# Two more receptances made early, four weight corrections moved to DMA, and mixing tables made one unit later

## The chip, the cores and the metric

The kernel runs on one core of one Trainium2 chip. Its metric is the device time of one execution in microseconds (us).

## The reference, cut to what matters

The input x has 2 sequences of 2048 times and 256 channels, 4096 tokens in all. All is in fp32. `F` stands for 512, the shared expert's width; there are 8 experts of width 256, and each token goes to the two of highest gate score.

```python
xn = layernorm(x)                                   # without scale and shift
k, v = xn @ key_w.T, xn @ value_w.T                 # time mixing
r = sigmoid(xn @ recep_w.T)                         # the "receptance"
# scan over time, per channel, state (aa, bb, pp):
#   wkv_t = (e1 * aa + e2 * v_t) / (e1 * bb + e2 + 1e-6)
#   e1, e2 from time_first and pp alone; the state decays by time_decay
mixed = (r * wkv) @ out_w.T
scores = softmax(xn @ gate_w.T + gate_b)            # 8 experts, top 2
expert_e(t) = (silu(t @ w1_e.T + b1_e) * (t @ w3_e.T + b3_e)) @ w2_e.T + b2_e
shared(t) = silu(t @ ws1.T + bs1) * (t @ ws3.T + bs3) @ ws2.T + bs2
out = x + mixed + sum of the two experts' results by their scores + shared(xn)
```

The scan as written never uses k, so its denominators and decay factors do not depend on x. They are tables over time and channel, which the kernel makes once: the mixing tables.

## The kernel before, in words

**Tiling.** The tokens are cut into 8 *steps* of 512 (256 times of both sequences). An fp32 product is made as three products of reduced-precision parts: each operand is cut into a high part (a rounding copy, by ScalarE) and a low part (what the rounding left, a subtraction, mostly by VectorE). "Cutting" below means this. A plain fp32 matmul exists too; `early_column` (L381) uses it.

**Three stages** follow each other, each with one stream of instructions for each engine: `route`, `run_experts`, `mix`. TensorE, VectorE, ScalarE, POOL and SP (which issues most DMAs) run their own streams in order and meet at semaphores. All orders are written out by hand.

**`route`.** SP loads x, then the experts' weights as 16 chunks of 128 x 768 (expert e, half k of the channels) into `w_lo`. Between the chunks it stores the normalized rows of each step (`xn_rows`, L449), from which the experts' tiles are gathered later. Which chunks go beside which step is `BESIDE`, their order `ARRIVAL`. The normalized rows lie in 4 buffers: step i writes (VectorE L726, ScalarE L518) where step i - 4 was, when that one's store has landed. TensorE turns each step (L600) and makes gate logits; VectorE chooses two experts for each token and gives each of the 8192 choices a slot; the counts and places in an expert come from small matmuls (L659 to L661), the token of each slot from comparisons and more small matmuls. With the tokens known, POOL gathers.

A change of variables needs the first row of each expert's up-weights subtracted from its other rows. For chunks 4 to 15 POOL issues an accumulating indirect DMA each (`less_first`, L390 to L398, 262 KB), when the chunk has arrived:

```python
nc.gpsimd.indirect_dma_start(
    out=w_parts[1][:, i, 0:2 * FF].bitcast(F32), out_offset=None, in_=nw_d,
    in_offset=bass.IndirectOffsetOnAxis(ap=index, axis=0), compute_op=ALU.add
).then_inc(s_less[e], 16)
```

For chunks 0 to 3 (`MADE = 4`) TensorE subtracts by matmul (`less`, `rest`) and ScalarE takes the result out (`made_hi`, `made_lo`), which makes the low part of the first 512 columns too; VectorE then cuts 256 columns of them where it cuts 768 of the others (`split_lo`, L427). ScalarE cuts chunks 4 to 12 (`split_hi`) in `route` and 13 to 15 at the start of `run_experts`. The values of step 7 (`last_v`) are made early in `route`, the receptance of step 6 (`last_r`, L383) at the start of `run_experts`, both with the raw weights `raw_v`, which SP loads late in `route`.

**`run_experts`.** The chosen tokens make 71 tiles of 128 rows, worked on in 36 *units* of two (unit 0 has one). In each unit a, every engine runs its part: POOL gathers for unit a + 4 or so ahead (L1022), TensorE turns the rows (L1093), multiplies up (L1099), turns the hidden product (L1119) and multiplies down (L1099); ScalarE and VectorE cut and combine (L1268 cuts x, L1277 makes the hidden product, L1284 cuts it). TensorE's order is fixed: turn_h(a), turn_x(a + 3), down(a - 1), up(a + 2).

Beside them go the mixing tables, eight of 256 times each, one in every four units. Each engine asks `v, r = divmod(a, 4)` and places its piece of table v by r: differences, exponentials (ScalarE), a scan, the denominator (POOL L1033 to L1036), four reciprocals (VectorE L1326, `invert`), a product (POOL L1041, `factors`), a store. VectorE's order in a unit is `hidden(a + 1)`, `cut_h(a)`, `cut_x(a + 3)`, then the tables' pieces. POOL's is:

```python
if a + AHEAD < DUOS: gather(a + AHEAD)
...
if a == A_LO: low_rows()                # A_LO = 24; L1047 to L1051, bias rows
...
if r == (1 if v == NPIECE else 2) and 0 < v <= NPIECE: factors(v - 1)
if r == 3 and v < NPIECE: denominator(v)
```

In the last units SP loads the raw mixing weights (`raw_vr`) and the columns of step 0 (`col`, L1012), and they are cut for the last stage.

**`mix`.** For each step: values (into `ps_v`), receptance (into `ps_r`, twelve matmuls L1571 to L1573), outputs of the step before (L1606, L1638 to L1640), the shared expert (`shared`, 96 matmuls). ScalarE applies tanh to the receptance (`receive`), VectorE multiplies with the scan, POOL gathers the experts' rows. Step 6 has no receptance to make and step 7 no values. In steps 6 and 7 and behind the last step the outputs come in another order (`outputs(..., last=True)`): the first two blocks of rows start before the last hidden product is cut. Steps 2 to 5 run in a loop of the engines.

## Time and profile before

| | |
|---|---|
| three runs | 464.21, 465.22, 469.5 us; median 465.22 |
| the profiled execution | 466.4 us; its span 464.7 us |
| mean granted TensorE clock | 0.981 |
| busy share: TensorE, VectorE, ScalarE, POOL | 96%, 79%, 52%, 51% |
| DMA traffic | 77.75 MB, mean 167 GB/s |

The span is what the profiler sees of the execution, from the first instruction to the last; the time holds 1.7 us more that lie around it. Stages in the span: `route` to about 62 us (the first gather), experts to about 263 us, mixing to the end. All timeline times are microseconds from the start of the span. In timelines and tables PE is TensorE's matmuls, PEld its weight loads, DVE VectorE, ACT ScalarE, SPq the DMAs that SP issues. A row of a timeline gives start, duration (of a group: first start to last end), engine, line, operation, output and inputs, shape, count, and in brackets the idle time before it with what ended it.

### The profile page before, as it was taken

The page shows a single profiled execution, that of the slowest core. Times are in us where ns is not written, and L with a number is a line of the kernel's source. Part 1 is how long each engine was busy: PE and PEld are TensorE (multiplying, and loading weights), DVE is VectorE, ACT ScalarE, POOL GpSimd, SP SyncE. Part 2 cuts the span into 40 slices and gives each one's busy share as a digit, 9 for nine tenths or more (in the row PEclk, how much of TensorE's full clock was granted, in tenths as well). Part 3 has the DMA queues.
Part 4 walks back from the last instruction along what each step waited for, and adds up shares of the span by engine and source line. Part 5 has one row for each costly group of instructions (what it writes and reads, how often), then busy time and mean ns, then how long its engine had stood idle before and what let it go on. Part 6 is the DMA issues. An engine that isn't in the chain of part 4 may idle for free.

```text
span 464.7 us, 8281 instructions
## 1 busy us (share of the span) xinstructions
PE 444.1 (96%) x2535; PEld 370.9 (80%) x2535; DVE 366.3 (79%) x680; ACT 240.9 (52%) x396; POOL 236.0 (51%) x224
## 2 busy tenths in 40 slices
PE   4898989979999999999999899999999999999997
PEld 4453657858888888888888778888898989898987
DVE  5968969878787887878766589996878778797963
ACT  4686835678668595967665633332423241333231
POOL 4234787544858666489846287743251607062000
PEclk9799879999999999999999999999999999999999
DMA  8999942356664865433473792635334453624011
GB/s 252 396 351 277 270 104 79 92 187 209 241 222 142 268 185 170 137 128 105 139 183 128 255 330 82 200 140 166 111 122 158 123 172 90 203 57 127 2 47 45
DMA packets 46145, 77.75 MB, mean 167 GB/s; under 512 B 5940, under 2 KB 32284, under 8 KB 46108
## 3 DMA queue, kind: packets, MB, share of 16 engines
q1 hardware_dynamic: 37196, 56.35, 34.9%
q0 software_dynamic: 8240, 20.88, 17.5%
q8 instruction: 21, 0.34, 0.3%
q10 hardware_dynamic: 672, 0.04, 0.1%
q14 instruction: 16, 0.13, 0.1%
HBM read 49.04 MB, written 28.21 MB: 166 GB/s over the span
## 4 chain that ended last, share of the span: by engine, by line
PE 44%; POOL 18%; issue 15%; DVE 9%; ACT 5%; DMA 5%; SPq 3%; POOLq 0%; DVEq 0%; ACTq 0%
POOL xg L1022 8%; PE ps_w L1571 5%; PE ps_w L1573 5%; PE ps_w L1572 5%; PE ps_w L1638 4%; PE ps_w L1640 4%; PE ps_w L1639 4%; PE ps_g L1099 4%; DMA w_lo<-w_all 3%; POOL den L1034 2%; PE ps_y L1099 2%; POOL den L1033 2%; SPq L436 2%; POOL col L1041 2%; POOL firsts L1041 2%
## 5 line engine op out<-in xcount | busy, mean ns | idle before, releaser
L1022 POOL DMA_INDIRECT xg<-xn_rows,tile_tok x71 | 72.8, 1026 | 20.2 <-issue 18.9
L1547 POOL DMA_INDIRECT yg<-expert_rows,rows x64 | 67.4, 1053 | 23.5 <-issue 17.1
L1099 PE MATMUL ps_g<-w_hi,x_hi 128*128 x142 | 56.2, 396 | 0.4 <-DVE x_lo L1268 0.4
L1099 PE MATMUL ps_g<-w_lo,x_hi 128*128 x142 | 56.3, 396 | 0.0
L1099 PE MATMUL ps_g<-w_hi,x_lo 128*128 x142 | 56.0, 395 | 0.0
L1682 ACT ACTIVATE sact<-ps_w,vec_b 128x512 f32<-128x512 f32 x32 | 22.0, 689 | 59.3 <-PE ps_w L1573 59.3
L1571 PE MATMUL ps_w<-col_hi,s_hi 128*128 128x512 f32 x128 | 50.7, 396 | 0.6 <-DVE shid L1796 0.4
L1573 PE MATMUL ps_w<-col_hi,s_lo 128*128 128x512 f32 x128 | 50.2, 392 | 0.0
L1572 PE MATMUL ps_w<-col_lo,s_hi 128*128 128x512 f32 x128 | 50.2, 392 | 0.0
L1099 PE MATMUL ps_y<-w_hi,h_hi 128*128 x142 | 43.1, 304 | 1.3 <-DVE h_lo L1284 1.3
L1277 DVE TENSOR_TENSOR hid<-ps_g,act 128x512 f32<-128x512 f32 (+1 forms) x36 | 23.7, 658 | 24.2 <-ACT act L1181 23.6
L1542 POOL COPY rows<-slots 128x8 int32<-128x8 int32 (+1 forms) x8 | 7.5, 933 | 65.4 <-DVE res L1766 56.6
L1099 PE MATMUL ps_y<-w_hi,h_lo 128*128 x142 | 40.0, 282 | 0.0
L1181 ACT ACTIVATE act<-ps_g 128x512 f32<-128x512 f32 (+1 forms) x36 | 21.3, 592 | 36.0 <-PE ps_g L1099 36.0
L1099 PE MATMUL ps_y<-w_lo,h_hi 128*128 x142 | 39.8, 281 | 0.0
L1796 DVE SCALAR_TENSOR_TENSOR shid<-ps_w,vec_b,sact 128x512 f32<-128x512 f32 x32 | 24.0, 751 | 17.8 <-ACT sact L1682 17.4
L1326 DVE RECIPROCAL den<-den 128x128 f32<-128x128 f32 x32 | 29.0, 930 | 11.2 <-POOL den L1036 10.9
L1639 PE MATMUL ps_w<-s_lo,s_hi 128*128 128x256 f32 x128 | 35.9, 280 | 0.0
L1638 PE MATMUL ps_w<-s_hi 128*128 128x256 f32 x128 | 35.9, 280 | 0.0
L1640 PE MATMUL ps_w<-s_hi,s_lo 128*128 128x256 f32 x128 | 35.9, 280 | 0.0
L1676 ACT ACTIVATE a_hi<-rw 128x1024 fp32r<-128x1024 f32 x8 | 8.5, 1059 | 48.6 <-PE ps_w L1640 43.8
L1099 PEld LDWEIGHTS ps_g<-w_hi,x_hi 128*128 128x128 f32 x142 | 26.7, 188 | 6.3 <-issue 1.3
(256 smaller groups left out, 1273.0 us busy)
## 6 DMA issues: line engine op xcount, KB each, us to landing
expert_rows<-y SPq DMA_DIRECT2D x35, 256.0 KB, 2.2
w_lo<-w_all SPq DMA_DIRECT2D x16, 384.0 KB, 9.3
table<-mix_tables SPq DMA_DIRECT2D x8, 768.0 KB, 6.5
xT<-x SPq DMA_DIRECT2D x16, 256.0 KB, 5.6
xn_rows<-xn SPq DMA_DIRECT2D x16, 256.0 KB, 8.3
xn_columns<-xT SPq DMA_DIRECT2D x8, 512.0 KB, 3.6
col<-xn_columns SPq DMA_DIRECT2D x8, 512.0 KB, 5.4
res<-x SPq DMA_DIRECT2D x16, 256.0 KB, 3.0
```

The lines of the kernel that those rows point to most:

```text
L1022: pool.indirect_dma_start(out=xg[b][:, t, :], out_offset=None, in_=xn_d[:, :], in_offset=bass.IndirectOffsetOnAxis(ap=tile_tok[:, first_ti ...
L1099: mm = nc.tensor.matmul(out, x[:, k, :], w[:, ds(e, 1), k, cols].rearrange("p o n -> p (o n)"), start=(k == 0 and n == 0), stop=(last and ...
L1277: nc.vector.tensor_tensor(hid[:, 0:n, :], ps_g[a % 2][:, 0:n, FF:2 * FF], act1[:, 0:n, :], ALU.mult).then_inc(c_h, 1)
L1326: ins = nc.vector.reciprocal(part, part)
L1547: pool.indirect_dma_start(out=yg[a.buf(2)][:, k, q, :], out_offset=None, in_=y_d[:, :], in_offset=bass.IndirectOffsetOnAxis(ap=picked[a.bu ...
L1571: nc.tensor.matmul(out, w_hi, x_hi, start=start, stop=False)
L1572: nc.tensor.matmul(out, w_hi, x_lo, start=False, stop=False)
L1573: return nc.tensor.matmul(out, w_lo, x_hi, start=False, stop=stop)
L1638: nc.tensor.matmul(out, hi[:, k, cols], w_hi[:, k, :], start=start, stop=False)
L1639: nc.tensor.matmul(out, hi[:, k, cols], w_lo[:, k, :], start=False, stop=False)
L1640: return nc.tensor.matmul(out, lo[:, k, cols], w_hi[:, k, :], start=False, stop=stop)
L1796: nc.vector.scalar_tensor_tensor(out=hid[m % 2][:], in0=ps_w[m % 2 * 2 + 1][:], scalar=vec_b3[:, m:m + 1], in1=act1[m % 2][:], op0=ALU.add ...
```

## The change

- `SPARED = (5, 4)`: the receptances of steps 5 and 4 are made in `route` by TensorE in plain fp32 (`early_column`, four halves), in place of `less` and `rest`. ScalarE takes them out into buffers that are still free (`spare`), SP stores them to DRAM ahead of the experts, and the mixing stage loads them back at its start. Steps 4 and 5 make no receptance, and outputs have the `last` order from step 4 on. The loop over steps 2 to 5 is written out.
- All 16 chunks are corrected by `less_first`: chunks 0 to 13 ahead of the gathers, 14 and 15 behind the fifth gather. Chunks arrive in their natural order. VectorE cuts all 768 columns of each chunk. ScalarE cuts chunks 0 to 13 in `route`, 14 and 15 in unit 1.
- `raw_v` has a buffer of its own and is loaded right behind x, ahead of the first chunk.
- `LATER = 1`: in `run_experts` every engine asks `divmod(a - LATER, 4)`, so the tables' pieces come one unit later, as do the first table's, the loading of `raw_vr` and that of the first columns. `A_ZERO`, `A_HI` and `A_LO` stay.

The diff, cut to its core:

```diff
+SPARED = (5, 4)
+SETS = len(SPARED)
...
-        MADE, BOTH, HIGH, LOW = 4, 4, 13, 4
+        HIGH, LOW = 14, 2
...
-        ARRIVAL = [0, 1, 4, 5, 2, 3] + list(range(6, E * KC))
+        ARRIVAL = range(E * KC)
         AHEAD, BESIDE = 2, (1, 2, 1, 2, 1, 2, 1, 2)
...
-        raw_v = xn[1][:].rearrange("p q c -> p (q c)")[:, 0:KC * 2 * C].rearrange("p (k n) -> p k n", k=KC)
+        raw_v = sb("raw_v", [P, KC, 2 * C], F32)
+        spare = [[t[:].rearrange("p t c -> p (t c)") for t in y],
+                 [firsts1[:, m].rearrange("p k t -> p (k t)") for m in range(KC)]]
...
-        def early_column(out, n0, i):
-            for k in range(KC):
+        def early_column(out, n0, i, ks=range(KC)):
+            for k in ks:
                 mm = nc.tensor.matmul(out, raw_v[:, k, n0:n0 + P], xT[i][:, k, :], start=k == 0, stop=k == KC - 1)
-            mm.then_inc(s_lastmm, 1)
+            if k == KC - 1:
+                mm.then_inc(s_lastmm, 1)
...
-            hi, lo = (w[:, i, 2 * FF if i < BOTH else 0:WALL] for w in w_parts)
+            hi, lo = (w[:, i, :] for w in w_parts)
...
+            sp.dma_start(raw_v[:], wvr.rearrange("(k p) n -> p k n", p=P)).then_inc(s_rawv, 16)
             arriving = iter(ARRIVAL)
             for _ in range(AHEAD):
                 load_w(next(arriving))
...
-            for i in range(MADE, E * KC):
+            for i in range(HIGH):
                 less_first(pool, i)
...
-            for i in range(MADE):
-                made_hi(act, i)
-            for i in range(4):
-                made_lo(act, i)
-                split(MADE + i)
-            nc.scalar.activation(early[:], gb[:], ACT.Silu)
-            for i in range(MADE + 4, HIGH):
+            for j in range(SETS):
+                for m in range(KC):
+                    act.wait_ge(s_lastmm, j * KC + m + 1)
+                    nc.scalar.activation(spare[j][m], ps_w[j * KC + m], ACT.Copy).then_inc(s_spare, 1)
+                    split(j * KC + m)
+            nc.scalar.activation(early_silu[:], gb[:], ACT.Silu)
+            for i in range(SETS * KC, HIGH):
                 split(i)
             act.wait_ge(s_terms, 3)
             for n in (0, 2):
                 ins = nc.scalar.activation(terms[:, :, n * E:(n + 1) * E].bitcast(F32R), dense[:], ACT.Copy)
...
-            pe.wait_ge(s_firsts, 2)
+            pe.wait_ge(s_rawv, 16)
             pe.wait_ge(s_Lg, len(GROUPS))
-            for i in range(MADE - 1):
-                less(i)
+            for m in range(KC):
+                early_column(ps_w[m], C + m * P, SPARED[0])
+            pe.wait_ge(s_Lc, len(GROUPS))
+            early_column(ps_w[KC], C, SPARED[1], [0])
             pe.wait_ge(s_upto, 1)
             nc.tensor.matmul(ps_total, ones[:], upto[:, :, NT - 1], start=True, stop=True).then_inc(s_cnt, 1)
             nc.tensor.matmul(ps_place, ones[:], upto[:].rearrange("p e j -> p (e j)"), start=True, stop=False)
             nc.tensor.matmul(ps_place, before[:], mask[:].rearrange("p e j -> p (e j)"), start=False, stop=True
                              ).then_inc(s_cnt, 1)
-            less(MADE - 1)
-            for i in range(4):
-                rest(pe, i)
+            early_column(ps_w[KC], C, SPARED[1], [1])
+            early_column(ps_w[KC + 1], C + P, SPARED[1])
...
+            sp.wait_ge(c_xhi, 1)
+            sp.wait_ge(s_spare, SETS * KC)
+            for j in range(SETS):
+                for m in range(KC):
+                    sp.dma_start(spare_d[j, m], spare[j][m]).then_inc(s_spared, 16)
             for a in range(DUOS + 1):
                 if a > 0:
                     store(a - 1)
-                v, r = divmod(a, 4)
...
-                v, r = divmod(a, 4)
-                if r == 2 and v < NPIECE:
+                v, r = divmod(a - LATER, 4)
+                if r == 2 and 0 <= v < NPIECE:
...
-                if a == 4 * LAST_V + 1:
+                if a == 4 * LAST_V + 1 + LATER:
                     sp.wait_ge(t_sides, NPIECE)
                     sp.dma_start(raw_vr[:], wvr).then_inc(c_vr, 16)
-                if a == 4 * LAST_V + 4:
+                if a == 4 * LAST_V + 4 + LATER:
                     assert (LAST_V - 1) % 2 == 0
                     sp.wait_ge(coef_stored, LAST_V * 16)
                     sp.dma_start(col0[:].rearrange("p k n -> p (k n)"), columns).then_inc(c_col, 16)
...
+                if a == 4:
+                    for i in range(HIGH, E * KC):
+                        less_first(pool, i)
             for a in range(DUOS):
-                v, r = divmod(a, 4)
+                v, r = divmod(a - LATER, 4)
                 if a + AHEAD < DUOS:
...
-            for i in range(HIGH, E * KC):
-                split_hi(act, i)
             cut_x(2)
             for a in range(DUOS):
-                v, r = divmod(a, 4)
+                v, r = divmod(a - LATER, 4)
                 silu(a + 1)
                 cut_h(a)
                 cut_x(a + 3)
                 if a == 0:
                     for m in range(KC):
                         receptance(m)
-                if a == 2:
+                if a == 1:
+                    for i in range(HIGH, E * KC):
+                        split_hi(act, i)
+                if a == 2 + LATER:
                     halves(0)
                     exps(0)
                 if r == 1 and 0 < v < NPIECE:
...
-                if a == 1:
+                if a == 1 + LATER:
                     grown(0)
                     differences(0)
-                if a == 2:
+                if a == 2 + LATER:
                     dve.wait_ge(t_dif, 1)
                     grown(1)
-                if a == 3:
+                if a == 3 + LATER:
                     scan_b(0)
                 if r == 0 and 0 < v <= NPIECE:
                     invert(v - 1, 0)
...
-            body(At(0, 0, 2), True, 2)
-            body(At(0, 1, 2), False, 2)
-            with eng.Fori(1, NSTEP // 2 - 1) as u:
-                body(At(u, 0, 2), False, 2)
-                body(At(u, 1, 2), False, 2)
-            body(At(NSTEP // 2 - 1, 0, 2), False, 1)
-            body(At(NSTEP // 2 - 1, 1, 2), False, 0)
+            for i in range(NSTEP):
+                body(At(i // 2, i % 2, 2), i == 0, min(2, NSTEP - 1 - i))
...
+            for j in range(SETS):
+                sp.dma_start(spare[j][:], spare_d[j].rearrange("k p n -> p k n")).then_inc(b_spare, 16)
...
-                if left != 1:
+                if a.i not in made:
...
-                    outputs(a.plus(-1), left < 2)
+                    outputs(a.plus(-1), a.i >= min(SPARED))
...
-                nc.scalar.activation(th[:].rearrange("p k b t -> p k (b t)"), (last_r if left == 1 else ps_r)[:], ACT.Tanh,
-                                     scale=0.5).then_inc(b_tanh, 1)
+                nc.scalar.activation(th[:].rearrange("p k b t -> p k (b t)"), made.get(a.i, ps_r)[:], ACT.Tanh, scale=0.5
+                                     ).then_inc(b_tanh, 1)
```

## Rows read from the trace of the kernel before

**Rows 1.** The page's first part: busy us, share of the span, instructions

```profile
PE 444.1 (96%) x2535; PEld 370.9 (80%) x2535; DVE 366.3 (79%) x680; ACT 240.9 (52%) x396; POOL 236.0 (51%) x224
```

**Rows 2.** Table by stretch: length, busy us (count) by engine, PE clock, DMA share, GB/s

```profile
16.00:24.00 8.00, 6.55 (x28) 3.49 (x26) 7.53 (x36) 6.79 (x15) 1.95 (x2) 0.96 1.06 398
38.00:46.00 8.00, 7.17 (x22) 2.66 (x20) 6.90 (x21) 6.59 (x12) 2.71 (x2) 1.00 1.10 252
54.00:56.00 2.00, 1.86 (x13) 1.30 (x11) 2.00 (x6) 1.45 (x3) 1.34 (x1) 0.56 1.05 180
94.00:104.00 10.00, 6.89 (x39) 5.29 (x38) 8.52 (x12) 6.54 (x12) 4.50 (x5) 1.00 0.57 211
285.00:430.00 145.00, 144.79 (x846) 127.31 (x845) 118.02 (x186) 44.31 (x63) 60.62 (x65) 1.00 0.44 137
```

**Rows 3.** Timeline of PE, the receptance of step 4: its first, and what follows

```profile
357.93 0.39 PE L1571 MATMUL ps_r<-col_hi,vr_hi 128*128 128x512 f32 x1
...
360.66 0.28 PE L1606 MATMUL ps_w<-rows_b,g_now 128*128 128x256 f32 x1
```

**Rows 4.** The corrections' line: count, ns min/median/max, first and last start; landing

```profile
L395 POOL DMA_INDIRECT w_lo<-first_rows,lane_i x6: 1534/1656/5333, 21.3 to 54.7; - x6
...
DMA to landing us min/median/max: 5.9/7.9/8.5
```

**Rows 5.** Timeline of all engines: step 7's normalization and its transposes

```profile
29.01 0.74 DVE L726 TENSOR_SCALAR xn<-xT,mv,rstd 128x256 f32<-128x256 f32 x2 [0.26 <-DMA xn_rows<-xn]
...
30.88 1.08 ACT L518 ACTIVATE xn<-xT,less,rstd 128x256 f32<-128x256 f32 x2
...
32.47 1.04 PE L600 MATMUL ps_T<-ident,xn 128*128 128x128 f32 x8
```

**Rows 6.** Timeline of POOL: the second correction, and the next five's first and last

```profile
23.76 1.55 POOL L395 DMA_INDIRECT w_lo<-first_rows,row_of  x1 [0.79 <-DMA w_lo<-w_all]
31.98 1.53 POOL L395 DMA_INDIRECT w_lo<-first_rows,lane_i  x1 [6.67 <-DMA w_lo<-w_all]
...
39.41 1.61 POOL L395 DMA_INDIRECT w_lo<-first_rows,lane_i  x1 [0.31 <-issue]
```

**Rows 7.** Timeline of PE: the counting matmul and one early half of step 6

```profile
43.44 0.18 PE L659 MATMUL ps_T<-upto,ones 128*128 128x8 bf16 x1 [0.83 <-DVE upto L804]
...
70.27 1.88 PE L383 MATMUL ps_y<-xT,xn 128*128 128x512 f32 x4
```

**Rows 8.** Timeline of DVE at the first units

```profile
64.45 1.42 DVE L427 TENSOR_TENSOR w_lo<-w_lo,w_hi 128x256 fp32r<-128x256 f32 x4
...
67.67 0.42 DVE L1268 TENSOR_TENSOR x_lo<-ps_x,x_hi 128x256 fp32r<-128x256 f32 x1 [1.27 <-ACT x_hi L1173]
68.01 2.69 DVE L427 TENSOR_TENSOR w_lo<-w_lo,w_hi 128x768 fp32r<-128x768 f32 x3
```

**Rows 9.** Timeline of POOL: factors of tables 3 and 4, denominator 5, bias rows

```profile
177.20 2.40 POOL L1041 TENSOR_TENSOR firsts<-firsts,den 128x1024 f32<-128x1024 f32 x1 [4.50 <-DVE den L1326]
...
197.64 2.40 POOL L1041 TENSOR_TENSOR col<-col,den 128x1024 f32<-128x1024 f32 x1 [4.49 <-DVE den L1326]
...
202.46 1.20 POOL L1033 TENSOR_TENSOR den<-firsts,s_b 128x512 f32<-128x512 f32 x1
...
208.33 2.88 POOL L1047 TENSOR_SCALAR rows<-rows,is_lo 128x1024 f32<-128x1024 f32 x1
...
214.12 2.41 POOL L1051 TENSOR_TENSOR rows_b<-rows,terms 128x1024 fp32r<-128x1024 f32 x1
```

**Rows 10.** Timelines of DVE and PE: reciprocals of tables 5 and 6

```profile
205.78 1.76 DVE L1326 RECIPROCAL den<-den 128x128 f32<-128x128 f32 x2 [1.89 <-POOL den L1036]
...
229.62 1.76 DVE L1326 RECIPROCAL den<-den 128x128 f32<-128x128 f32 x2 [2.86 <-POOL den L1036]
...
232.68 0.63 PE L1119 MATMUL ps_h<-ident,hid 128*128 128x128 f32 x4 [0.67 <-DVE h_lo L1284]
```

**Rows 11.** Timelines of SP and ACT: the first columns loaded and cut

```profile
246.63 0.47 SPq L1012 DMA_DIRECT2D col<-xn_columns  x1
...
255.43 1.05 ACT L1258 ACTIVATE col_hi<-col 128x1024 fp32r<-128x1024 f32 x1
```

More of the change, by code:

```diff
@@ L330, in route @@
         s_w = [sem(f"s_w{i}") for i in range(E * KC)]
-        s_less = {e: sem(f"s_less{e}") for e in range(MADE // KC, E)}
-        s_dif = sem("s_dif")
-        s_dlo = sem("s_dlo")
-        s_both = sem("s_both")
-        s_low = sem("s_low")
-        s_firsts = sem("s_firsts")
+        s_less = {e: sem(f"s_less{e}") for e in range(E)}
         s_negl = sem("s_negl")
@@ L372, in route @@
         s_lastv = sem("s_lastv")
+        s_spare = sem("s_spare")
+        s_spared = sem("s_spared")
         s_upto = sem("s_upto")
@@ L550, in scalar @@
             nc.scalar.activation(before[:], before_f[:], ACT.Copy, scale=-1.0)
-            nc.scalar.activation(minus[:], ident[:], ACT.Copy, scale=-1.0)
             turned(At(0, 0, NSTEP))
@@ L869, in route @@
                                                    (HIGH, LOW), (split_hi, split_lo, store_columns, less_first),
-                                                   (s_lastmm, last_r, early_column))
+                                                   (s_lastmm, last_r, early_column),
+                                                   (s_spare, s_spared, spare))
 def run_experts(nc, kept, placed, xn_d, y_d, y, y_stored, firsts1, coef_stored, tab_d, vec_tf, vec_td, ident, tile_tok, tile_exp,
-                w_hi, w_lo, terms, bias, vr, col, loads, b_all, wvr, columns):
+                w_hi, w_lo, terms, bias, vr, col, loads, b_all, wvr, columns, spare_d):
     with ExitStack() as ctx:
@@ L1077, in gpsimd @@
                     factors(v - 1)
-                if r == 3 and v < NPIECE:
+                if r == 3 and 0 <= v < NPIECE:
                     denominator(v)
@@ L1394, in vector @@
                         invert(v - 1, 3)
-                if r == 3 and v < LAST_V:
+                if r == 3 and 0 <= v < LAST_V:
                     differences(v + 1)
@@ L1423, in mix @@
         x_lo = [col_lo0, sb("col_lo1", [P, KC, STEP], F32R)]
+        spare = [sb(f"spare{j}", [P, KC, STEP], F32) for j in range(SETS)]
         res = [sb(f"res{b}", [P, Q, C], F32) for b in range(2)]
@@ L1472, in mix @@
         b_slot = sem("b_slot")
-        e_y, e_yc, e_wlo, e_gT, e_rows, s_lastv, last_r = over
+        b_spare = sem("b_spare")
+        e_y, e_yc, e_wlo, e_gT, e_rows, s_lastv, last_r, s_spared = over
+        made = {i: spare[j] for j, i in enumerate(SPARED)} | {NSTEP - 2: last_r}
         xv = x.rearrange("b (i h p) c -> i p b h c", h=HALF, p=P)
@@ L1666, in receive @@
                     act.wait_ge(s_lastv, 2 * KC)
+                elif a.i in made:
+                    act.wait_ge(b_spare, SETS * 16)
                 else:
-                    act.wait_ge(b_r, a.i + 1 if left else a.i)
+                    act.wait_ge(b_r, sum(i not in made for i in range(a.i + 1)))
                 at_least(act, b_rw, a.i)
-                nc.scalar.activation(th[:].rearrange("p k b t -> p k (b t)"), (last_r if left == 1 else ps_r)[:], ACT.Tanh,
-                                     scale=0.5).then_inc(b_tanh, 1)
+                nc.scalar.activation(th[:].rearrange("p k b t -> p k (b t)"), made.get(a.i, ps_r)[:], ACT.Tanh, scale=0.5
+                                     ).then_inc(b_tanh, 1)
             def cut_a(a):
```

69 lines of the change are left out of this document (18 added, 51 removed).

## The prediction

> **What bounds the kernel now.** I read the engine totals first [rows 1]: TensorE is busy for 96% of the span, so time is won only where its work shrinks or its few idle places fill. The table by stage [rows 2] says where these are. From 285 to 430 us, in the mixing steps, it is busy 144.79 of 145 us: there a microsecond of matmul taken out is a microsecond of time, as long as nothing else becomes late. From 94 to 104 us it idles 3.11 us; this is where the first mixing table is made. At the start, from 16 to 46 us, the columns to read are the last two: the DMA engines are full throughout, but carry 398 GB/s from 16 to 24 us and only 252 from 38 to 46. The second stretch is the one in which first-row corrections land; the accumulating DMAs use engine time badly. Where one correction runs alone, from 54 to 56 us, they carry 180 GB/s.
>
> **The change, part by part.**
>
> *Steps 4 and 5 lose their receptances.* The block of twelve matmuls of step 4 runs from 357.93 to 360.66 [rows 3], 2.73 us; step 5 has the same one. With no idle time around them [rows 2] this gives **-5.5**. What hides behind them now is the cutting of the step before: the outputs that follow wait for it, and the change gives these steps the output order that steps 6 and 7 have, whose stretch shows no idle time. VectorE is busy 118 of 145 us, 20.9 of a step of 25.7, and would have 22.9: if its waits return, less is won. Bounds -3 and -5.5; I take the upper, since steps 6 and 7 run so already. Unrolling the loop I cost at nothing: it shows no gap on TensorE.
>
> *Four more corrections by DMA, and the raw weights ahead.* Corrections of chunks 0 to 3 go from TensorE and ScalarE to POOL's queue; its first one is issued at 21.3 today, for the third chunk to arrive, and the median one lands 7.9 us after issue [rows 4]. The first chunk arrives earlier, so I put the four added ones at some 19.5 to 25 us. What is then in the sync queue is the normalized rows of steps 2 and 3. Step 7 writes into the buffer of step 3 and waits for that store: VectorE was released at 29.01 by it [rows 5]. Each correction moves 128 rows of 2 KB, 262 KB, which at 180 GB/s is 1.46 us of all engines; four are 5.8. The raw weights, 524 KB, at 398 GB/s are 1.3. If all of it goes ahead of store 3, step 7 is released at 29.0 + 7.1 = 36.1 us. ScalarE's half then takes 1.08, and the transposes of step 7 start at about 37.4 in place of 32.47 [rows 5]: **+4.9**, passed on whole, since scores, choice, slots and gathers follow one from the other. Bounds: with only the raw weights ahead, 30.3 + 1.1 still fits under 32.47, so 0; the other end is 4.9 plus whatever store 2 loses, 6. I take 4.9 because of 38 to 46 us: of five corrections, issued 32 to 39.4 [rows 6], some four and a half land there, 1.2 MB of the 2.0 that 252 GB/s make in 8 us. Stores and weights had the other 0.8 MB, where the rate of 16 to 24 us would have given them 3.2: a quarter. The last chunks come later too, and ScalarE now cuts 12 and 13 ahead of the gate terms; against that, gather 0 no longer queues behind chunks 14 and 15. I set these two against each other (-1.3 to +3).
>
> The Trainium skill (DMA: Bandwidth & Descriptors, section Queues, rings and completion order) says that a DMA engine takes turns, packet by packet, between the queues that have work. An estimate by that rule: equal turns leave the stores half the rate while corrections run, say from 24.5 us on. The sync queue's work up to store 3 is then 29.0 - 24.5 and 1.3 for the raw weights, 5.8 us; 4 of it pass in 8 us of sharing and 1.8 after that, so store 3 is done at 34.3 rather than 36.1, and the sum below is 1.8 lower. The rows gave the stores less than half, so I stay with them.
>
> *TensorE and ScalarE in the routing.* Out go the matmuls that corrected four chunks; in come four blocks of early columns (two halves of two steps), each like the one of 1.88 us at 70.27, 7.5 in all [rows 7]. They stand before and behind the counting matmuls, which waited 0.83 for VectorE at 43.44: at full clock they fit between 38 and 47 us, and the comparing of slots is what VectorE does next in any case. Cost 0; if that cover goes, at most the 1.9 of one block. The evictions and stores of the four halves run behind ScalarE's cutting and beside gathers; 0.
>
> *VectorE's cutting of weights.* Chunks 0 to 3 are now cut over all 768 columns: four short pieces (1.42) become two long ones ahead of the first x_lo, where 1.27 us of waiting covers the rest; but five long pieces rather than three stand between x_lo(0) and the first hidden product [rows 8]. A long piece is 2.69 / 3 = 0.90: **+1.8** to the second unit, with nothing behind it until TensorE is full. Bounds +0.4 and +2.2. Chunks 14 and 15 come late, but are cut a unit before their use.
>
> *Tables one unit later, at their beginning.* VectorE's differences no longer sit behind the last splits, and ScalarE finds them ready. The 3.11 idle us of 94 to 104 have two causes, this wait and ScalarE's own run of exponentials with its table loads; I take half, **-1.6** (0 to -3.1).
>
> *Tables one unit later, in the middle.* POOL's three operations for the bias rows (L1047 to L1051) stay at unit 24. Today the denominator of table 5 is POOL's last work of unit 23; shifted, it belongs to unit 24, behind them. Working: factors come every 20.44 us, four units, so a unit is 5.11 [rows 9]. Factors of table 4 move to 202.75, the denominator would start 4.82 later, at 207.57, as now; but the rows take 208.33 to 216.53, 8.2 us, and go first. VectorE stands at the reciprocals, in order, with the next unit's hidden product and h_lo queued behind, for which TensorE's transposes wait. Today it waits 1.89 there [rows 10] and TensorE does not notice; it will wait 10.1. How much is absorbed: at 229.62 it waited 2.86 from 226.76, which is 2.43 behind the pattern (203.89 + 20.44 = 224.33), and TensorE idled 0.67 at 232.68. So 2.43 + 2.86 - 0.67 = 4.62 is free and 10.1 - 4.6 = 5.5 is idle. The 0.67 of table 6 goes, as its denominator is no longer late: **+4.8**, bounds 0 (should POOL be far ahead) and 7.
>
> *At the end* the first columns are loaded a unit later: issued at 246.63 and cut at 255.43 today [rows 11], 8.8 us, of which 3.7 are left; and two reciprocals move to unit 34. **+0.5** (0 to 2). The reloading of spare columns, 1 MB, follows the first loads of the mixing stage and is needed four steps later: 0.
>
> **Sum:** -5.5 + 4.9 + 1.8 - 1.6 + 4.8 + 0.5 = +4.9. The profiled execution took 466.4 us (span 464.7), so it would be 471.3; it lies 1.2 above the median of 465.2, on which scale I forecast **470.1**.
>
> **Rivals.** *The corrections leave the stores alone* (chance 0.26). For it: the correction issued at 23.76 was under way too [rows 6] and store 3 still came by 29.0. Then 4.9 falls away: 465.2, no change, and not slower; decided by whether step 7's transposes start before 33 us. *Neither crowding nor the bias rows count* (0.15): the sum is then -4.8, 460.4, a little under 1% faster, and with the whole 3.1 at 94 us 458.9. *The clock falls in the new gaps* (0.17): from 54 to 56 us TensorE was granted 0.56, near the lower of its two levels, 1.2 of 2.4 GHz, though it was busy 1.86 of 2 us [rows 2], in small matmuls that wait for VectorE's comparisons. Two gaps of 5 us, each with 4 us at half clock behind it, lose 2 each: 474. The Trainium skill (TensorE: Matmul & The Clock Gate, Part 1) has the clock halved after idling, which speaks for this case. *VectorE binds steps 4 to 6* is within the bounds above, 2.5 more. That the change does nothing for the mixing steps I give no chance: their matmuls are gone.
>
> **Numbers.** The forecast has 0.42; its own range is 466.5 to 474. About 1% (4.7 us) is what a measurement of this kernel can tell from no change, so the forecast lies just beyond that bound, and somewhat more than half of its chance with it; with the clock case, slower gets 0.45. Same, from the rest of the forecast and the first rival, 0.40; faster, mostly the second, 0.15. For 8 in 10 I go from 462 to 476.
>
> **What would show it.** Right: no receptance matmuls in steps 4 and 5 and steps of about 23 us; L726's last pair and step 7's transposes at 36 to 38 us; one idle gap of some 5 us on TensorE about unit 27, released by VectorE behind the denominator, with L1047 to L1051 running just ahead of that; less idle time where the first table is made. Wrong: transposes of step 7 by 33 us (the crowding step), a denominator that is ready when the reciprocals come (the bias rows step), or idle TensorE in steps 4 to 6 (the cover step).

## The result

| | before | changed |
|---|---|---|
| median of the runs | 467.04 us (464.21 to 469.5) | 478.43 us (477.34 to 480.34) |
| profiled execution, its span | 466.4, 464.7 us | 478.64, 476.9 us |
| mean granted TensorE clock | 0.981 | 0.971 |

The changed kernel is **slower by 2.7%**: ratio 1.0273, 95% interval 1.0234 to 1.0313. The medians in the table, of four runs each, give 1.0244; the kernel before reached a median of 465.7 on the chip of the first experiments. The forecast was 470.1, a little slower; the time lies above its range of 462 to 476. The sign was right, the forecast size less than half of the measured one.

The engine totals of the changed kernel, in the columns of [rows 1]:

```profile
PE 442.3 (93%) x2503; PEld 370.0 (78%) x2503; DVE 365.7 (77%) x678; ACT 237.9 (50%) x390; POOL 247.1 (52%) x228
```

TensorE is busy for 1.8 us less in a span that is 12.2 us longer: it idles 14 us more, and some of its busy time is slow clock (below). To find where it arises I read the same milestone in both traces, the turning of each unit's hidden product on TensorE (L1119 before, L1090 after). The difference, after minus before, in us:

| milestone | late by | gained or lost since the line above |
|---|---|---|
| step 7's transposes | 4.85 | +4.85 |
| tokens known (VectorE's tok_f) | 4.47 | -0.38 |
| gate terms | 8.31 | +3.84 |
| first up matmul, unit 0 | 7.33 | -0.98 |
| hidden turn, unit 0 | 9.28 | +1.95 |
| unit 6 | 7.63 | -1.65 |
| unit 19 | 9.63 | +2.00 |
| unit 27 | 16.09 | +6.46 |
| unit 28 | 18.20 | +2.11 |
| unit 35 | 17.17 | -1.03 |
| end of the span | 12.2 | -4.97 |

**Start.** The corrections go out from 18.94 us (timeline of POOL, changed kernel); five of them to 26.61, where the kernel before had issued two (21.27 and 23.76):

```profile
18.94 1.70 POOL L396 DMA_INDIRECT w_lo<-first_rows,lane_i  x1 [5.72 <-DMA w_lo<-w_all]
...
26.61 1.54 POOL L396 DMA_INDIRECT w_lo<-first_rows,lane_i  x1 [0.31 <-issue]
...
56.62 7.82 POOL L396 DMA_INDIRECT w_lo<-first_rows,lane_i  x1 [3.16 <-DMA w_lo<-w_all]
64.75 1.54 POOL L396 DMA_INDIRECT w_lo<-first_rows,row_of  x1 [0.30 <-issue]
```

Step 7 then waits for the store of step 3, 2.83 us behind a wait of 3.64 for that of step 2 (timelines of VectorE, TensorE and ScalarE):

```profile
35.47 0.74 DVE L689 TENSOR_SCALAR xn<-xT,mv,rstd 128x256 f32<-128x256 f32 x2 [2.83 <-DMA xn_rows<-xn]
...
37.32 1.04 PE L576 MATMUL ps_T<-ident,xn 128*128 128x128 f32 x8
...
70.19 1.58 ACT L403 ACTIVATE w_hi<-w_lo 128x768 fp32r<-128x768 f32 x2 [8.84 <-DMA w_lo<-first_rows,row_of]
...
72.41 0.42 DVE L823 TENSOR_TENSOR terms<-dense,terms 128x256 f32<-128x256 f32 x1 [4.54 <-ACT terms L562]
...
75.00 0.42 DVE L1242 TENSOR_TENSOR x_lo<-ps_x,x_hi 128x256 fp32r<-128x256 f32 x1
```

35.47 and 37.32 answer to 29.01 and 32.47 in [rows 5]. The last three lines are the second loss: ScalarE stood 8.84 us at the cutting of chunks 12 and 13, in order ahead of the gate terms, and VectorE 4.54 us for those. The correction of chunk 12 had taken 7.82 us to issue.

**Middle.** The rows of unit 24 and behind (POOL, VectorE, TensorE), which answer to [rows 9, 10]:

```profile
218.15 2.88 POOL L1015 TENSOR_SCALAR rows<-rows,is_lo 128x1024 f32<-128x1024 f32 x1
...
223.94 2.40 POOL L1019 TENSOR_TENSOR rows_b<-rows,terms 128x1024 fp32r<-128x1024 f32 x1
226.30 1.18 POOL L1001 TENSOR_TENSOR den<-firsts,s_b 128x512 f32<-128x512 f32 x1
...
229.55 1.76 DVE L1300 RECIPROCAL den<-den 128x128 f32<-128x128 f32 x2 [10.57 <-POOL den L1004]
...
232.60 1.09 PE L1090 MATMUL ps_h<-ident,hid 128*128 128x128 f32 x4 [6.31 <-DVE h_lo L1258]
```

The bias rows go first, the denominator behind them, VectorE waits 10.57 us and TensorE idles 6.31. The table by stretch (columns of [rows 2]) shows what the forecast had as a rival only: behind the gap TensorE ran at the lower clock. At the routing's end (60 to 66 us) it did so too, but that is no loss of the change: the kernel before was granted 0.50 there from 56 to 64 us. The 0.66 of 72 to 82 us is new; before, the first units had 1.00.

```profile
24.00:32.00 8.00, 5.18 (x23) 2.78 (x21) 4.01 (x21) 3.52 (x9) 3.45 (x3) 1.00 1.11 255
60.00:66.00 6.00, 5.74 (x30) 3.92 (x29) 4.50 (x11) 1.35 (x2) 5.70 (x2) 0.50 0.14 23
72.00:82.00 10.00, 7.93 (x25) 5.52 (x26) 9.50 (x20) 3.79 (x9) 8.17 (x7) 0.66 0.57 185
...
229.00:234.00 5.00, 1.40 (x7) 1.43 (x8) 4.41 (x7) 2.05 (x3) 3.81 (x5) 0.63 0.20 65
234.00:240.00 6.00, 6.00 (x29) 5.41 (x28) 5.77 (x10) 1.52 (x3) 2.85 (x4) 0.74 0.46 139
```

**End.** Steps 4 and 5 of the mixing stage begin at 372.36 and 395.60 and end at 418.55 (first values of steps 4, 5 and 6 on TensorE):

```profile
372.36 0.39 PE L1546 MATMUL ps_v<-col_hi,vr_hi 128*128 128x512 f32 x1
...
395.60 0.39 PE L1546 MATMUL ps_v<-col_hi,vr_hi 128*128 128x512 f32 x1
...
418.55 0.39 PE L1546 MATMUL ps_v<-col_hi,vr_hi 128*128 128x512 f32 x1
```

That is 23.24 and 22.95 us, where the kernel before took 25.68 and 25.41 (the same rows of TensorE, before):

```profile
355.20 0.39 PE L1571 MATMUL ps_v<-col_hi,vr_hi 128*128 128x512 f32 x1
...
380.88 0.40 PE L1571 MATMUL ps_v<-col_hi,vr_hi 128*128 128x512 f32 x1
...
406.29 0.39 PE L1571 MATMUL ps_v<-col_hi,vr_hi 128*128 128x512 f32 x1
```

4.9 us are won. What is lost lies all ahead of the mixing stage.

### The profile page after: what moved, and what is told of

The parts are those of the page before. It is cut to its first block, busy times and chain, and to the rows that moved or that the text cites. A ratio compares the mean times of both kernels' runs of the same rounds, so it can differ in the third digit from the quotient of the medians.

```text
span 476.9 us, 7976 instructions
## 1 busy us (share of the span) xinstructions
PE 442.3 (93%) x2503; PEld 370.0 (78%) x2503; DVE 365.7 (77%) x678; ACT 237.9 (50%) x390; POOL 247.1 (52%) x228
## 4 chain that ended last, share of the span: by engine, by line
PE 55%; DVE 13%; issue 10%; POOL 9%; DMA 5%; ACT 4%; SPq 3%; DVEq 0%; POOLq 0%; ACTq 0%
PE ps_g L1070 12%; PE ps_y L1070 6%; PE ps_w L1546 5%; PE ps_w L1548 5%; PE ps_w L1547 5%; PE ps_w L1615 4%; PE ps_w L1613 4%; PE ps_w L1614 4%; POOL xg L990 4%; DMA w_lo<-w_all 3%; SPq L432 2%; PE ps_x L1064 2%; PE ps_h L1090 2%; DVE stats L668 2%; DMA w_lo<-first_rows,row_of 1%
## 5 line engine op out<-in xcount | busy, mean ns | idle before, releaser
L1522 POOL DMA_INDIRECT yg<-expert_rows,rows x64 | 69.0, 1078 | 23.7 <-issue 17.1
L1517 POOL COPY rows<-slots 128x8 int32<-128x8 int32 x8 | 6.7, 839 | 54.2 <-DVE res L1743 50.3
```

The costliest lines, as they stand in the source:

```text
L1522: pool.indirect_dma_start(out=yg[a.buf(2)][:, k, q, :], out_offset=None, in_=y_d[:, :], in_offset=bass.IndirectOffsetOnAxis(ap=picked[a.bu ...
```

## The experiments

Each is measured against the kernel before, run on the same chip. The profiled start of one kernel varies by up to 2.5 us from execution to execution (unit 0 is late by 9.28 to 11.80 in four kernels with the same routing stage), so positions are compared inside one trace where possible. Milestones are "late by" as in the table above.

### Bias rows behind the denominator again

```diff
-        A_ZERO, A_ROWS, A_HI, A_LO = 13, 18, 22, 24
+        A_ZERO, A_ROWS, A_HI, A_LO = 13, 18, 22, 25
```

> The changed kernel with the bias rows' three operations one unit later (unit 25), so that the denominator of table 5 goes ahead of them again; all else as changed. Theory: VectorE's wait of 10.57 us for that denominator and TensorE's gap of 6.31 us at unit 27 come from POOL doing the bias rows first, and the half clock behind the gap costs 2.1 more. Then the gap goes and the time falls by 7.5 to 9 us, from 478.4 to about 470. Rival: the shifted tables themselves bring the gap (reciprocals one unit later meet POOL's gathers): a gap of over 3 us stays and the time is within 2 us of 478.4.

Measured: 472.86 us, ratio 1.017 (1.0101 to 1.024). The big gap is gone: units 19 to 29 are late by a constant 10.02, and VectorE's wait at those reciprocals is 2.45 us. The time fell by 5.6 us, less than the 7.5 to 9 expected: the bias rows now delay the next table, so two small waits come, before unit 31 and unit 32, where the changed kernel gives 1.03 back.

```profile
221.83 1.76 DVE L1300 RECIPROCAL den<-den 128x128 f32<-128x128 f32 x2 [2.45 <-POOL den L1004]
...
242.35 0.63 PE L1090 MATMUL ps_h<-ident,hid 128*128 128x128 f32 x4 [0.33 <-DVE h_lo L1258]
...
248.69 0.63 PE L1090 MATMUL ps_h<-ident,hid 128*128 128x128 f32 x4 [0.88 <-DVE h_lo L1258]
```

### The same order in the kernel before

```diff
-        A_ZERO, A_ROWS, A_HI, A_LO = 13, 18, 22, 24
+        A_ZERO, A_ROWS, A_HI, A_LO = 13, 18, 22, 23
```

> The kernel before with nothing changed but the bias rows' three operations, one unit earlier (unit 23), so that they stand ahead of the denominator of table 5. Theory: that order alone makes VectorE wait some 10 us and TensorE idle 5.5 to 6.5 us at unit 26, with 2 us of half clock behind it, and table 6's 0.67 goes: 6.5 to 8.5 us slower, 1.014 to 1.018 of before. Rival: the gap needs the tables' shift: within 1 us of before.

Measured: 472.57 us, ratio 1.0131 (1.0106 to 1.0155), just under the expected 1.014 to 1.018. The order alone makes the gap, with no shifted tables:

```profile
212.93 1.76 DVE L1326 RECIPROCAL den<-den 128x128 f32<-128x128 f32 x2 [9.99 <-POOL den L1036]
...
215.98 1.09 PE L1119 MATMUL ps_h<-ident,hid 128*128 128x128 f32 x4 [5.37 <-DVE h_lo L1284]
```

Against the unit before, unit 26 is 5.54 us late, unit 27 another 2.52 (half clock), and table 6 gives back 0.85: 7.0 by unit 35. Together the two runs settle this step: undone it goes, done alone it comes.

### All pieces of the bias rows one unit later

```diff
-        A_ZERO, A_ROWS, A_HI, A_LO = 13, 18, 22, 24
+        A_ZERO, A_ROWS, A_HI, A_LO = 14, 19, 23, 25
```

> The changed kernel with all four pieces of the bias rows (clearing, loading, rounding, the three operations, and with them VectorE's mask) one unit later, so that they stand to the tables as before the change. Theory: besides the gap at unit 27, the mask now falls in a unit in which VectorE also scans and POOL multiplies, and this makes the 1.1 us of idle TensorE at units 17 and 18; then this kernel is 1 to 1.8 us below the one with only the three operations moved, at about 468.5. Rival: the idle time at units 17 and 18 comes from the tables alone: this kernel is within 0.6 us of that one, and the waits of 0.27 and 0.85 us for h_lo stay.

Measured: 472.16 us (469.32 to 475.34), ratio 1.0108 (1.0037 to 1.018). The runs scatter too far to tell 0.7 us from the first experiment, and the median is above the expected 468.5, but the trace answers: units 7 to 29 are late by a constant 10.3, so the 1.8 us that the changed kernel loses between units 16 and 19 are gone. There VectorE's mask stands ahead of the hidden product in a unit that also has a scan and a reciprocal. It meets POOL's product, so that an instruction on 128x1 elements takes 2.20 us, and what follows then meets POOL's denominator (174.48 to 177.88):

```profile
169.66 2.41 POOL L1009 TENSOR_TENSOR col<-col,den 128x1024 f32<-128x1024 f32 x1 [3.38 <-DVE den L1300]
...
169.88 2.20 DVE L1310 TENSOR_TENSOR is_lo<-is_lo 128x1 f32<-128x1 f32 x1
...
174.00 3.40 DVE L1279 SCALAR_TENSOR_TENSOR raw_vr<-s_p,vec_tf 128x256 f32<-128x256 f32 x2
```

The third line took 1.52 us in the tables before and behind. The meeting with POOL alone is not the loss: in the kernel before the mask met the denominator and took 1.82 us (160.99), in this run again (176.42), but one unit after the scan, and TensorE did not wait. At the end this run lost 2.4 us of its own: TensorE's last wait was 3.71 us and not 1.29, with VectorE's col_lo at 2.91 us in front of the last hidden product (VectorE and TensorE):

```profile
267.55 2.91 DVE L1339 TENSOR_TENSOR col_lo<-col,col_hi 128x1024 fp32r<-128x1024 f32 x1 [0.60 <-ACT col_hi L1232]
...
271.21 0.57 PE L1070 MATMUL ps_y<-w_hi,h_hi 128*128 x1 [3.71 <-DVE h_lo L1258]
```

### The tables back at their old units

```diff
-        LATER = 1
+        LATER = 0
```

> The changed kernel with the tables at their old units; early receptances, corrections and loads as changed. Theory: the shift itself costs 8.8 at unit 27 and 1.8 at units 16 to 18 and gives back 1.65 at the first table and 0.8 at table 6, so without it the time is about 469.5 (469 to 471). Rival: the shift is nearly neutral, and the loss lies in the routing stage and in clock states: 475 or more.

Measured: 472.1 us, ratio 1.0132 (1.0082 to 1.0182); the profiled run 470.93; 1.1 above the expected 469 to 471, and under the rival's 475. Every unit from 0 to 35 is late by 9.4 to 9.5, and the end by 4.5: without the shift the whole loss is the routing stage, and 4.9 comes back in the mixing stage. The two waits of the first table (1.59 and 1.54) are there again, where the changed kernel has only one, of 1.52:

```profile
106.38 0.63 PE L1090 MATMUL ps_h<-ident,hid 128*128 128x128 f32 x4 [1.59 <-DVE h_lo L1258]
...
113.38 0.63 PE L1090 MATMUL ps_h<-ident,hid 128*128 128x128 f32 x4 [1.54 <-DVE h_lo L1258]
```

### The corrections held until step 7 is normalized

```diff
             pool.wait_ge(s_lane, 3)
+            pool.wait_ge(s_xna, NSTEP)
```

> The changed kernel with POOL's corrections held until step 7 is normalized; all else as changed. Theory: the corrections that start at 18.9 us take the DMA engines from the stores of steps 2 and 3, and that makes step 7's transposes 4.85 us late (37.3 in place of 32.5). Held back, they start at 33.0 to 34.5 (the raw weights alone remain ahead of the stores), so the second scores come 3 to 4.5 us earlier. What the hold costs later is open: if the last corrections still land with the last chunks, the time falls by 3 to 4 us; if they then trail, the wait for chunks 12 and 13 grows and the time moves by less than 1.5. Rival: the raw weights and the natural order of the chunks delay the stores; step 7's transposes stay at 36.5 or later.

Measured: 479.1 us, ratio 1.0274 (1.0243 to 1.0305): no gain in time, the second of the two outcomes. The mechanism is shown all the same: step 7's transposes are at 32.56, in the kernel before at 32.47 [rows 5]. The tokens are known at 59.60 and not 64.45. Then the terms lose all of it:

```profile
32.56 1.04 PE L577 MATMUL ps_T<-ident,xn 128*128 128x128 f32 x8
...
50.22 9.38 POOL L396 DMA_INDIRECT w_lo<-first_rows,row_of  x1 [0.30 <-issue]
...
67.28 0.99 POOL L991 DMA_INDIRECT xg<-xn_rows,tile_tok  x1 [0.30 <-issue]
...
72.86 0.43 DVE L824 TENSOR_TENSOR terms<-dense,terms 128x256 f32<-128x256 f32 x1 [9.84 <-ACT terms L563]
```

The tenth correction was issued while VectorE compares slots and took 9.38 us; four more and the first gather stood behind it. The ninth, issued two microseconds before in the same comparisons, had taken 1.72.

### The raw weights later

```diff
-            sp.dma_start(raw_v[:], ...)            # behind x
...
+                if a.i == 3:
+                    sp.dma_start(raw_v[:], ...)    # behind the store of step 3
```

> The changed kernel with the raw weights loaded behind the store of step 3's rows in place of right behind x; all else as changed. Theory (the corrections crowd): step 7's transposes come 1.3 us earlier, the raw weights' own share, near 36, and the early columns still find their weights; the time falls by 0 to 1.3 us. Rival (the raw weights are the cause): the transposes come at 34 or before.

Measured: 480.54 us, ratio 1.0312 (1.0275 to 1.0349). Transposes at 36.56, 0.8 earlier than in the changed kernel and 0.5 or more earlier than in the five other kernels that load them first and start their corrections as changed (37.01 to 38.97): the raw weights are a small part of the crowding, as the theory had it. The time rose by some 2 us instead of falling. 2.4 us of the profiled run (483.31, the slowest of the four) are the long last wait, 3.71 us, that the bias rows' run had too; why the others rose stays open.

### ScalarE's cutting of chunks 12 and 13 behind the terms

```diff
-            for i in range(SETS * KC, HIGH):
+            for i in range(SETS * KC, HIGH - KC):
                 split(i)
...
+            for i in range(HIGH - KC, HIGH):     # experts' stage, behind cut_x(1)
+                split_hi(act, i)
             cut_x(2)
```

> The changed kernel with ScalarE's cutting of chunks 12 and 13 moved from ahead of the gate terms to the experts' stage, behind the second unit's x; all else as changed. Theory: the terms stood 8.84 us behind ScalarE's wait for the correction of chunks 12 and 13, and that is 3.9 us of the 9.3 that the first hidden turn is late, with up to 1.7 more because TensorE then runs at half clock. Then terms come at about 68.5 us in place of 72.4 and the time falls by 3.5 to 5.5 us, to about 474. Rival: the gathers and VectorE's wide cutting bind there anyway, so terms come early but the first hidden turn stays within 1.5 us of 86.4, and the time within 1.5 us of 478.4.

Measured: 478.55 us, ratio 1.0278 (1.0225 to 1.0332), with no gain. Terms came at 68.29 and the first x_lo 3.6 us earlier, as expected, but the hidden turn of unit 0 only 1.9 earlier (late by 7.38), and the median did not move. Two things took the rest, 3.67 us from the first up matmul to the first hidden turn. One is the five wide pieces (128x768 each) ahead of the first hidden product: the second x_lo follows the first by 5.01 us, 3.43 before. The other is TensorE's clock: after 1.71 us of idling it was granted 0.50 to 0.69 from 76 to 80 us, and four plain fp32 matmuls of step 6's receptance took 3.46 us (1.88 before [rows 7]):

```profile
68.29 0.42 DVE L823 TENSOR_TENSOR terms<-dense,terms 128x256 f32<-128x256 f32 x1 [0.69 <-ACT terms L562]
...
71.38 0.42 DVE L1244 TENSOR_TENSOR x_lo<-ps_x,x_hi 128x256 fp32r<-128x256 f32 x1 [0.41 <-ACT x_hi L1144]
71.72 4.42 DVE L409 TENSOR_TENSOR w_lo<-w_lo,w_hi 128x768 fp32r<-128x768 f32 x5
...
76.02 3.46 PE L383 MATMUL ps_y<-xT,raw_v 128*128 128x512 f32 x4 [1.71 <-issue]
```

### The first gathers ahead of corrections 12 and 13

The edit before, and:

```diff
-            for i in range(HIGH):
+            for i in range(HIGH - KC):
                 less_first(pool, i)
...
                 gather(a)
+                if a == 1:
+                    for i in range(HIGH - KC, HIGH):
+                        less_first(pool, i)
```

> The changed kernel with ScalarE's cutting of chunks 12 and 13 behind the second unit's x, and POOL's corrections of chunks 12 and 13 behind the gathers of the first two units. Theory: the correction that took 7.82 us while VectorE compared slots stands ahead of the first gather and holds it by 1.6 us or more (66.6, tokens ready at 65.0); with the gathers first, gather 0 comes at 65.3, the first rows turn 1.3 us earlier, and the first hidden turn is 1 to 2 us earlier than where only the cutting was moved (84.5). Rival: VectorE's cutting binds the first units and the hidden turn stays within 0.7 us of that.

Measured: 479.54 us, ratio 1.0266 (1.0227 to 1.0305). The first gather is at 66.06 with POOL idle for 12.16 us ahead of it, and unit 0's hidden turn is late by 5.29, the expected 2 us less. But the gather did not do it: the first x_lo and the first up matmul stand where they stood when only the cutting was moved (71.36 and 72.04; there 71.38 and 72.05). The 2.1 us come behind them, where TensorE kept its full clock and the same four fp32 matmuls took 1.98 us and not 3.46; it had idled 1.04 us before them in place of 1.71, and why stays open (POOL, VectorE, TensorE):

```profile
66.06 0.99 POOL L990 DMA_INDIRECT xg<-xn_rows,tile_tok  x1 [12.16 <-DVE tile_tok L810]
...
71.36 0.42 DVE L1247 TENSOR_TENSOR x_lo<-ps_x,x_hi 128x256 fp32r<-128x256 f32 x1
...
75.19 1.98 PE L383 MATMUL ps_y<-xT,raw_v 128*128 128x512 f32 x4 [1.04 <-issue]
```

Unit 3 gives 1.55 back, waiting for a gather that stands behind the last corrections, and the median did not move. One part of the routing at a time does not reach the end: the next one is close behind.

### The routing stage mended in all its parts

Held corrections (until step 5 is normalized), gathers ahead of corrections 12 and 13, ScalarE's cutting of these two in unit 0, and VectorE's cutting spread:

```diff
+            pool.wait_ge(s_xna, 6)
...
+            split_lo(dve, 0)                     # while the tokens are waited for
             dve.wait_ge(s_hotmm, PAIRS // BATCH)
...
-            for i in range(LOW, 7):
+            for i in range(LOW, 6):
                 split_lo(dve, i)
             hidden(0)
             cut_x(1)
-            for i in range(7, 12):
+            for i in range(6, 10):
```

Chunks 10 to 13 are then cut in unit 0. (The edits of the two experiments before are left out of the cut.) First with the tables at their old units:

> The changed kernel with the tables at their old units and the routing stage mended: corrections held until step 6's predecessor (step 5) is normalized, those of chunks 12 and 13 behind two gathers, ScalarE's cutting of these two in unit 0, VectorE's cutting spread so that four wide pieces, not five, stand ahead of the first hidden product. Theory: the routing stage's 9.3 us are the crowded stores (4.9), the terms behind ScalarE's wait (3.9) and half clock (up to 1.7), each now taken away, so the first hidden turn is within 1.5 us of that of the kernel before (77.1), and what is left is the two receptances, 4.9 of 5.5 us: 460 to 462.5, 0.988 to 0.992 of before. Rival: corrections on DMA cost the stage its engine time whatever their order: the first hidden turn stays over 3 us late and the time is 464 or more.

Measured: 464.33 us, ratio 0.9959 (0.9937 to 0.9981). The routing loss is gone: unit 0 is late by 0.42 in place of 9.28, transposes at 32.27. The time is above the expected range, as units 2 to 4 lose 2.5 us, to waits for wide cutting (0.56), a gather (0.28) and the first table.

Then with the tables and all bias rows one unit later:

> The same mended routing stage, with the tables one unit later as changed, and all pieces of the bias rows one unit later with them. Theory: the shift then costs nothing in the middle and gives 1.65 at the first table and 0.8 at table 6: 1 to 2.5 us below the kernel with the tables at their old units, 458.5 to 460.5, unless the later columns cost up to 2.4 at the end, where two runs showed a wait of 3.71 us in place of 1.29. Rival: the shift gives nothing once the gap is gone: within 0.7 us of that kernel.

Measured: 464.62 us (461.05 to 465.95), ratio 0.9959 (0.9933 to 0.9984): above the expected 458.5 to 460.5, by the condition that was named. Units 6 to 29 are at +0.1 and unit 30 at -0.74, but the last wait is 3.71 again.

### The end mended too

VectorE's cut_h of the last unit ahead of col_lo, and chunks 10 and 11 cut by ScalarE behind the second unit's x:

```diff
                 hidden(a + 1)
+                cut_h(a)
                 if a == DUOS - 1:
                     dve.wait_ge(c_whi, 2)
                     nc.vector.tensor_tensor(col[2][:], ...)
-                cut_h(a)
```

> The kernel with the mended routing stage and tables and bias rows one unit later, with two more edits: VectorE cuts the last hidden product before the first columns instead of behind them, and ScalarE cuts chunks 10 and 11 behind the second unit's x. Theory: TensorE's last wait in the experts' stage (3.71 us, and 1.29 in the kernel before) is VectorE standing at the columns' low part while the last hidden product waits behind it; with the order turned it is under 0.5 us, and the gate terms (65 us there, 2.8 of it a wait for ScalarE) come 1.5 to 2 us earlier: 459 to 461.5, 0.986 to 0.990 of before. Rival: the mixing stage's first values then wait for the columns' low part as long as the hidden product did before: 463 to 464.5, within 1 us of that kernel.

Measured: 460.29 us (460.11 to 462.18), ratio **0.9903** (0.9889 to 0.9918): 1% faster than the kernel before. The gate terms come 4.07 us behind the tokens and not 6.15 as in the run above. The last wait is 0.64, a little over the expected 0.5, and 0.73 comes for the columns, 1.4 in all for 3.71:

```profile
257.12 0.38 PE L1075 MATMUL ps_y<-w_hi,h_hi 128*128 x1 [0.64 <-DVE h_lo L1267]
...
259.54 0.51 PE L1555 MATMUL ps_v<-col_hi,vr_hi 128*128 128x512 f32 x1 [0.73 <-DVE col_lo L1349]
```

## Why the prediction was right or wrong

**Steps 4 and 5: right.** 4.9 of 5.5 us. The cover held: TensorE is busy 46.17 of the 46.19 us of these two steps. The other 0.6 is no idle time and stays untraced.

**Crowding: right in mechanism, and in size with some luck.** +4.85 forecast as 4.9, transposes at 37.32 forecast as 37.4; held corrections bring 32.56. In the parts, step 7 was released at 35.47 and not at 36.1, and the way from there to the transposes took 1.85 us and not 1.3; those five other kernels released it at 35.6 to 36.1. By the rule of the Trainium skill (DMA: Bandwidth & Descriptors, section Queues, rings and completion order), as the prediction worked it out, the release would have come at 34.3. The traces lie behind that, nearer to the unequal rows: from 24 to 32 us, at 255 GB/s in all, stores and weights moved 0.97 MB and the corrections 1.07, where 16 to 24 us of the kernel before had given the former 3.14. That is three tenths; the forecast had a quarter, equal turns half.

**The last chunks: the step that failed.** The prediction set "the last chunks come later too, and ScalarE now cuts 12 and 13 ahead of the gate terms" against an earlier gather, and took nothing (-1.3 to +3). It cost 3.84 between the tokens and the gate terms, and the gather gained nothing: it comes at 66.59 in place of 62.14, as late as the tokens, since the corrections of chunks 12 and 13 now stand ahead of it. What was missed is that a correction issued while VectorE compares can be held until the comparisons are over, and then delays the correction behind it, the gathers and ScalarE in turn. The row was in the trace before (5.33 us, the maximum in [rows 4]) and the sum had no term for it. ScalarE's order has its part: with the cutting moved behind, the terms came 4.11 us after the tokens, as before (4.12), though the correction took 7.55 us; in the five kernels with the corrections and ScalarE's order as changed they come 7.96 to 8.25 us after. How much the late chunks would cost in the old order without the hold is not shown: no run has that.

**Wide cutting: right, a little under the +1.8.** With five pieces the second x_lo follows the first 1.6 to 1.7 us later than with three, in the changed kernel and in both runs with the cutting moved. In the one of these that kept its full clock (gathers first) all of it, and nothing else, reaches the first hidden turn. In the changed kernel the second unit's up matmuls start 0.25 us after their x_lo, while TensorE is at half clock until 80 us; both end at about the same time, and the 1.95 us of unit 0 cannot be shared out between them. In the mended kernel, with four pieces and one moved forward, unit 0 is late by 0.42.

**Tables, first: right, the size by luck.** -1.65, forecast -1.6: of two waits of about 1.5 us one went. The forecast took half of the idle time because it saw two causes, not because a row gave the half.

**Tables, middle: right mechanism, too small.** VectorE's wait 10.57 (forecast 10.1), TensorE's idle time 6.31 (5.5). Two terms were missing: the half clock behind the gap (+2.1), which stood as a rival at 0.17 with 2 us for each of two gaps, although such a gap was part of the forecast itself; and the mask in the scan's unit (+1.8 of the +2.0 between units 6 and 19), which I did not look for: of the bias rows' pieces only POOL's were checked against the shift.

**End: as good as nothing**, forecast +0.5; but it is where the runs with mended middle lost 2.4.

By these terms the sum goes from +4.9 to +12.2: +3.8 terms, +2.1 half clock behind the gap, +1.8 the mask, and small ones that come to -0.4.

## What to carry to other kernels

When work is shifted against other work, list every piece that stays and check it against each engine's order at the new place: one found conflict (bias rows and denominator) hid a second of the same kind (the mask). When a forecast contains a gap of 5 us and more on TensorE, the slow clock behind it belongs to the sum, at the price that the nearest gap shows, and not to a rival. And indirect DMAs issued by POOL should not be left pending when VectorE begins a dense series on its own memory, since one of them can be held to the end of it: order them ahead of it, or behind the work that waits for it.

## What the runs showed of the hardware

**POOL's DMA issue and VectorE's series.** In twelve of the thirteen kernels a correction issued in the slot comparisons was held: it ended 1.40 to 1.42 us after VectorE's last instruction on two operands in its memory, however long it had waited. So it was at 59.99 and 58.57 us before, 64.44 and 63.03 in the changed kernel, 59.60 and 58.18 with held corrections. That is also when VectorE has the tokens, but the mended kernel tells the two apart: there a cutting piece stands last, and the correction ended at 60.09, 1.42 after it (58.67), the tokens being known at 59.23. A free one takes 1.54, so a held one looks as if it began when the series ends. But nine others that were issued in the same comparisons went through in 1.5 to 1.9 us, one of them in the kernel before, 2.5 us ahead of the held one; what decides stays open (POOL and VectorE, before, and then the mended kernel with tables back):

```profile
52.12 1.58 POOL L395 DMA_INDIRECT w_lo<-first_rows,row_of  x1 [0.30 <-issue]
54.66 5.33 POOL L395 DMA_INDIRECT w_lo<-first_rows,lane_i  x1 [0.96 <-DMA w_lo<-w_all]
58.13 0.44 DVE L845 TENSOR_TENSOR gated<-hot_tile,tok_b 128x568 f16<-128x568 f16 x1
...
55.13 4.96 POOL L396 DMA_INDIRECT w_lo<-first_rows,row_of  x1 [7.63 <-DMA w_lo<-w_all]
57.73 0.94 DVE L409 TENSOR_TENSOR w_lo<-w_lo,w_hi 128x768 fp32r<-128x768 f32 x1
```

The Trainium skill (SBUF — State Buffer, section SBUF: two separate sides) says that VectorE and GpSimd (POOL) share a pair of ports, and that a VectorE instruction with two operands in that memory holds it for the whole instruction against a GpSimd instruction that reads there, as a correction does for its row numbers. The held ones agree, and were kept out over many separate instructions back to back; how nine others got in, no run shows.

**VectorE behind POOL.** The reverse holds too. 128x1 elements took 2.20 us beside POOL's 2.41 us product, and both ended at 172.07. In the run with all bias rows later col_lo took 2.91 us, with POOL's product ending 1.07 us before its end (1.23 without the product beside it). The Trainium skill (same page, section Who interferes with whom) names two operands in that memory as the condition, beside a POOL instruction that reads it; both instructions have two.

**The clock.** In the token matmuls TensorE was granted 0.50 (1.2 of 2.4 GHz) from 60 to 66 us, though busy 5.74 of 6 us; the kernel before shows the same. Behind 6.31 us of idling it was granted 0.50 from 231 to 237 us and 0.96 from 237 to 239, and the unit behind the gap took 2.1 us longer; 2.5 in the kernel before with bias rows first. Four plain fp32 matmuls took 3.46 us at 0.50 to 0.69 and 1.98 at 1.00.
